# Five scattered tiles on two sums, three row sums combined by DVE and PE, and selection matrices made in quarters

## The reference, cut to what matters

```python
# x: (1024, 256); 16 experts with hidden size 256
logits = x @ router_weight.T + router_bias
top_val, top_idx = jax.lax.top_k(logits, 4)
router_scores = zeros.at[token, top_idx].set(softmax(top_val))
gate_up = einsum('th,ehd->etd', x, gate_up_proj) + bias
out = einsum('etd,edh->eth', (up + 1) * glu(gate), down_proj) + down_bias
out = (out * router_scores.T[:, :, None]).sum(axis=0)      # a sum over experts, per token
result = x + layernorm(out)
```

## Time and profile before

| | us |
|---|---|
| median of 3 runs | 511.5 (510.91, 511.5, 516.53) |
| the profiled execution's own time | 514.36 |
| its span in the trace | 512.6 |

### The profile page before, as it was taken

The page is one execution under the profiler, slowest core; times in us unless marked ns, Lnnn a source line. Parts: engine busy times, 40 slices in busy tenths (PEclk is TensorE's granted clock), DMA queues, the critical chain, the costliest instruction groups (busy, mean ns, idle before and its releaser), DMA issues. The chain is left out here.

```text
span 512.6 us, 11665 instructions
## 1 busy us (share of the span) xinstructions
PE 469.9 (92%) x3466; PEld 439.8 (86%) x3466; DVE 356.6 (70%) x1258; ACT 325.5 (63%) x815; POOL 248.5 (48%) x236
## 2 busy tenths in 40 slices
PE   6699999999999999999999999789889999999933
PEld 3698898999899999999999998588789999998833
DVE  4698788686866686876687797376666767668605
ACT  4878986768586767576676656546458665655402
POOL 1888884444222355435442245016835555554363
PEclk9999999999999999999999999998899999999967
DMA  8357651999400000000365346533655555655742
GB/s 240 108 188 234 213 182 35 374 369 370 159 1 1 22 25 36 23 26 36 127 212 179 127 140 212 165 115 67 139 104 102 93 106 92 105 91 79 160 127 84
DMA packets 63406, 67.49 MB, mean 132 GB/s; under 512 B 4529, under 2 KB 58225, under 8 KB 63345
## 3 DMA queue, kind: packets, MB, share of 16 engines
q1 hardware_dynamic: 54896, 55.79, 34.6%
q0 software_dynamic: 7872, 10.49, 11.8%
q10 hardware_dynamic: 576, 0.46, 0.3%
HBM read 32.63 MB, written 34.10 MB: 130 GB/s over the span
## 5 line engine op out<-in xcount | busy, mean ns | idle before, releaser
L514 POOL TENSOR_TENSOR by_sin<-by_sin,rope_sin 128x512 f32<-128x512 f32 x64 | 82.4, 1288 | 148.5 <-ACT by_sin L659 148.5
L1522 PE MATMUL bank<-xgT,gu_now 128*128 128x128 f32 x752 | 95.1, 281 | 3.6 <-ACT xgT L659 1.7
L659 ACT ACTIVATE by_sin<-bank 64x512 f32<-64x512 f32 x128 | 75.7, 592 | 34.1 <-PE bank L1324 32.6
L612 POOL DMA_INDIRECT sum_d<-y,xg x44 | 68.5, 1558 | 58.7 <-ACT y L787 55.1
L1522 PEld LDWEIGHTS bank<-xgT,gu_now 128*128 128x128 f32 x752 | 90.9, 198 | 5.0 <-DVE gu_now L1143 3.8
L681 ACT ACTIVATE prob<-score,row_bias 128x128 f32<-128x128 f32 (+1 forms) x128 | 57.1, 447 | 47.2 <-DVE row_bias L971 47.1
L1324 PE MATMUL bank<-xT_h,qk_h 128*128 128x256 f32 x256 | 77.5, 303 | 4.3 <-DVE qkT L961 1.7
L971 DVE CUSTOM_DVE_ANT_0 score<-bank,mask 128x128 f32<-128x128 f32 (+1 forms) x128 | 40.3, 351 | 52.2 <-issue 52.2
L1324 PE MATMUL bank<-xT_h,qk_l 128*128 128x256 f32 x256 | 72.2, 282 | 0.0
L1324 PE MATMUL bank<-xT_l,qk_h 128*128 128x256 f32 x256 | 72.1, 282 | 0.0
L1324 PEld LDWEIGHTS bank<-xT_h,qk_h 128*128 128x128 f32 x256 | 48.8, 191 | 5.1 <-POOL qk_l L499 3.4
(11 more groups left out here) (182 smaller groups left out, 1178.6 us busy)
## 6 DMA issues: line engine op xcount, KB each, us to landing
rows_d<-blank SPq DMA_DIRECT2D x32, 576.0 KB, 7.5
gu_w<-_L_ffn_gate_up_proj_dram SPq DMA_DIRECT2D x16, 512.0 KB, 5.7
xg<-rows_d SPq DMA_DIRECT2D x47, 144.0 KB, 2.6
dn_w<-in_L_ffn_down_proj_dram SPq DMA_DIRECT2D x16, 256.0 KB, 3.0
sum_d<-blank SPq DMA_DIRECT2D x2, 1152.0 KB, 9.9
raw_qk<-in_L_attn_wq_dram SPq DMA_DIRECT2D x16, 128.0 KB, 3.6
raw_qk<-in_L_attn_wk_dram SPq DMA_DIRECT2D x16, 128.0 KB, 3.7
raw_v<-in_L_attn_wv_dram SPq DMA_DIRECT2D x8, 256.0 KB, 2.7
```

The lines of the kernel that those rows point to most:

```text
L514: pool.tensor_tensor(v, v, rope_sin[:, :].unsqueeze(1).broadcast_to([P, 2, T]), ALU.mult).then_inc(pool_sin, 1)
L612: pool.indirect_dma_start(out=sum_d[i % SUMS], out_offset=bass.IndirectOffsetOnAxis(ap=xg[:, i % XG, TOKEN:TOKEN + 1].bitcast(U32), axis=0 ...
L659: return sc.activation(out, in_, ACT.Copy)
L1522: m = pe.matmul(ps_gu[i % 2][:, (2 * s + r) * P:(2 * s + r + 1) * P], gu_now[:, i % 2, k, s, r * P:(r + 1) * P], xgT[:, i % XT, k, :], sta ...
```

## The change

In the loop and at its end:

- Scatters 39 to 43 go to sums 0 and 1 in turn (`HOME`), so each of 41 to 43 waits for the scatter two before it, no longer three before. Sum 2 has its last scatter with tile 38, and SP loads it to `sum_a` as soon as that has landed and the row loads are issued.
- The last two sums are loaded in four parts each (two for `sum_b` before).
- The additions on POOL go. DVE adds `sum_b` to `sum_a` (`add_two`); PE adds that and, by an own pair of products, `sum_c` (`add_sum`).
- PE does the products of the first two late tiles for all units ahead of any sum, then unit by unit those of the third tile and the two sums.
- The token numbers of the late tiles come by three small loads of their own (`late_token`, 8 bytes a row), and the 0/1 comparisons are made in quarters of 256 columns, one after each of tiles 20 to 31.
- `down(46)` writes to another PSUM bank (that of `gate_up(45)`), and waits for DVE's reading of it rather than for tile 44's late rows. Tile 44's `late_low` stands in the loop, after `gated(46)`.
- The last token tile's output is stored by ACT on its own queue, in a DMA of 128 KB, beside SP's.

```diff
+        ps_out = [ps_y[i % 2] for i in range(TILE_MAX - 1)] + [ps_gu[TILE_MAX % 2]]
...
-        ENDING = [(LAST + k) % SUMS for k in range(SUMS)]
+        TWO = LAST - 5
+        HOME = [i % SUMS if i < TWO else (TWO + (i - TWO) % 2) % SUMS for i in range(LAST)]
+        def added(i):
+            return 16 * HOME[:i + 1].count(HOME[i])
...
-            for i in range(EARLY + 3, TILE_MAX):
+            for i in range(EARLY + 3, EARLY + XG):
                 load_rows(i)
-            for i, to, signal in ((ENDING[0], sum_a, dma_first), (ENDING[1], sum_b, dma_second)):
-                sp.wait_ge(dma_sum[i], 16 * ((LAST - 1 - i) // SUMS + 1))
-                for u in range(2):
-                    sp.dma_start(to[:, 4 * u:4 * u + 4, :], sum_rows[i][:, 4 * u:4 * u + 4, :]).then_inc(signal[u], 16)
-            sp.wait_ge(dma_sum[ENDING[2]], 16 * ((LAST - 1 - ENDING[2]) // SUMS + 1))
-            for u in range(4):
-                sp.dma_start(sum_c[:, 2 * u:2 * u + 2, :], sum_rows[ENDING[2]][:, 2 * u:2 * u + 2, :]).then_inc(dma_third[u], 16)
-            for u in range(4):
+            for j in range(LATE):
+                row = sp.value_load(entry(LAST + j, 1), min_val=0, max_val=BLANK)
+                sp.dma_start(late_token[:, j, :], rows_d[bass.ds(row, P), TOKEN:TOKEN + 2].bitcast(I32)).then_inc(dma_token, 16)
+            for i in range(EARLY + XG, TILE_MAX):
+                load_rows(i)
+            sp.wait_ge(dma_sum[HOME[TWO - 1]], added(TWO - 1))
+            for u in range(2):
+                sp.dma_start(sum_a[:, 4 * u:4 * u + 4, :], sum_rows[HOME[TWO - 1]][:, 4 * u:4 * u + 4, :]).then_inc(dma_first[u], 16)
+            for i, to, signal in ((LAST - 2, sum_b, dma_second), (LAST - 1, sum_c, dma_third)):
+                sp.wait_ge(dma_sum[HOME[i]], added(i))
+                for u in range(4):
+                    sp.dma_start(to[:, 2 * u:2 * u + 2, :], sum_rows[HOME[i]][:, 2 * u:2 * u + 2, :]).then_inc(signal[u], 16)
+            for u in range(3):
                 sp.wait_ge(act_moe, 2 * u + 2)
                 sp.dma_start(out_rows[:, 2 * u:2 * u + 2, :], sum_b[:, 2 * u:2 * u + 2, :]).then_inc(dma_out, 16)
-            sp.wait_ge(dma_out, 16 * 4)
+            sp.wait_ge(act_moe, TILES - 1)
+            sp.dma_start(out_rows[:, TILES - 2, :], sum_b[:, TILES - 2, :]).then_inc(dma_out, 16)
+            sp.wait_ge(dma_out, 16 * 5)
...
-                    pool.wait_ge(dma_sum[i % SUMS], 16 * (i // SUMS))
-                pool.indirect_dma_start(out=sum_d[i % SUMS], out_offset=bass.IndirectOffsetOnAxis(
+                    pool.wait_ge(dma_sum[HOME[i]], added(i) - 16)
+                pool.indirect_dma_start(out=sum_d[HOME[i]], out_offset=bass.IndirectOffsetOnAxis(
                     ap=xg[:, i % XG, TOKEN:TOKEN + 1].bitcast(U32), axis=0), in_=y[:, i % YR, :], in_offset=None,
-                    compute_op=ALU.add).then_inc(dma_sum[i % SUMS], 16)
+                    compute_op=ALU.add).then_inc(dma_sum[HOME[i]], 16)
...
-            def add_second(u):
-                pool.wait_ge(dma_first[u // 2], 16)
-                pool.wait_ge(dma_second[u // 2], 16)
-                tiles = slice(2 * u, 2 * u + 2)
-                pool.tensor_tensor(sum_a[:, tiles, :], sum_a[:, tiles, :], sum_b[:, tiles, :], ALU.add).then_inc(pool_first, 1)
-            def add_third(u):
-                pool.wait_ge(dma_third[u], 16)
-                pool.wait_ge(pool_first, u + 1)
-                tiles = slice(2 * u, 2 * u + 2)
-                pool.tensor_tensor(sum_a[:, tiles, :], sum_a[:, tiles, :], sum_c[:, tiles, :], ALU.add).then_inc(pool_whole, 1)
             for u in range(4):
-                add_second(u)
-            add_third(0)
-            add_third(1)
-            add_third(2)
-            power("moe", 0)
-            add_third(3)
-            for u in range(1, 4):
                 power("moe", u)
...
+            sc.wait_ge(act_moe, TILES)
+            sc.dma_start(out_rows[:, TILES - 1, :], sum_b[:, TILES - 1, :]).then_inc(dma_out, 16)
...
-            def rows_to_tokens(j):
-                i = LAST + j
-                dve.wait_ge(dma_xg[i % XG], 16 * (i // XG + 1))
-                chain(dve.tensor_copy(token[:, j:j + 1], xg[:, i % XG, TOKEN:TOKEN + 1].bitcast(I32)))
-                chain(dve.tensor_scalar(from_end[:, j, :], full_edge[:, :], token[:, j:j + 1], None, ALU.subtract))
-                dve.tensor_tensor(turn[:, j, :, :], from_end[:, j, :].unsqueeze(2).broadcast_to([P, TILES, P]),
-                                  countdown[:, :].unsqueeze(1).broadcast_to([P, TILES, P]), ALU.is_equal).then_inc(dve_turn, 1)
+            def token_rows():
+                dve.wait_ge(dma_token, 16 * LATE)
+                dve.tensor_copy(token[:, :], late_token[:, :, 0]).then_inc(dve_token, 1)
+                dve.wait_ge(dve_token, 1)
+                dve.tensor_tensor(from_end[:, :, :], full_edge[:, :].unsqueeze(1).broadcast_to([P, LATE, TILES]),
+                                  token[:, :].unsqueeze(2).broadcast_to([P, LATE, TILES]), ALU.subtract).then_inc(dve_token, 1)
+                dve.wait_ge(dve_token, 2)
+            def which_token(j, u):
+                tiles = slice(2 * u, 2 * u + 2)
+                dve.tensor_tensor(turn[:, j, tiles, :], from_end[:, j, tiles].unsqueeze(2).broadcast_to([P, 2, P]),
+                                  countdown[:, :].unsqueeze(1).broadcast_to([P, 2, P]), ALU.is_equal).then_inc(dve_turn, 1)
...
-                dve.scalar_tensor_tensor(out=late_l[:, j, :], in0=ps_y[i % 2][:, 0:M], scalar=xg[:, i % XG, bass.ds(e + M, 1)],
...
                     experts[i + 1] = place_gu(i + 1)
                 clamp(i, experts[i])
                 gated(i)
-                if LAST - 4 <= i < LAST - 4 + LATE:
-                    rows_to_tokens(i - LAST + 4)
-            for j in range(LATE):
+                if i == EARLY + 10:
+                    token_rows()
+                if EARLY + 10 < i <= EARLY + 10 + 4 * LATE:
+                    which_token((i - EARLY - 11) // 4, (i - EARLY - 11) % 4)
+                if i - 2 >= LAST:
+                    late_low(i - 2 - LAST, experts[i - 2])
+            for j in range(LATE - 2, LATE):
                 late_low(j, experts[LAST + j])
+            def add_two(u):
+                dve.wait_ge(dma_first[u // 2], 16)
+                dve.wait_ge(dma_second[u], 16)
+                tiles = slice(2 * u, 2 * u + 2)
+                dve.tensor_tensor(sum_a[:, tiles, :], sum_a[:, tiles, :], sum_b[:, tiles, :], ALU.add).then_inc(dve_two, 1)
+            for u in range(4):
+                add_two(u)
...
                 e = pe.value_load(entry(i, 0), min_val=0, max_val=E - 1)
                 pe.wait_ge(dve_act, i + 1)
-                if i >= 2:
+                if i == TILE_MAX - 1:
+                    pe.wait_ge(dve_up, i)
+                elif i >= 2:
                     pe.wait_ge(act_y, i - 1)
-                if i - 2 >= LAST:
-                    pe.wait_ge(dve_late, i - 1 - LAST)
+                    if i - 2 >= LAST:
+                        pe.wait_ge(dve_late, i - 1 - LAST)
                 for r in range(2):
-                    m = pe.matmul(ps_y[i % 2][:, 0:M], act[:, i % AR, r, :],
+                    m = pe.matmul(ps_out[i][:, 0:M], act[:, i % AR, r, :],
...
                 if i > EARLY:
                     down(i - 2)
-            def add_late(u, j, first=False, last=False):
-                pe.wait_ge(dve_turn, j + 1)
+            def add_late(u, j, first=False):
+                pe.wait_ge(dve_turn, 4 * j + u + 1)
                 pe.wait_ge(dve_late, j + 1)
                 for s in range(2):
                     for rows in (late_h, late_l):
-                        m = pe.matmul(ps_sum[u][:, s * M:(s + 1) * M], turn[:, j, 2 * u + s, :], rows[:, j, :],
-                                      start=first and s == 0 and rows is late_h, stop=last and s == 1 and rows is late_l,
-                                      skip_group_check=True)
+                        pe.matmul(ps_sum[u][:, s * M:(s + 1) * M], turn[:, j, 2 * u + s, :], rows[:, j, :],
+                                  start=first and s == 0 and rows is late_h, stop=False, skip_group_check=True)
+            def add_sum(u, rows, last=False):
+                for s in range(2):
+                    m = pe.matmul(ps_sum[u][:, s * M:(s + 1) * M], ident[:, :], rows[:, 2 * u + s, :], start=False,
+                                  stop=last and s == 1, skip_group_check=True)
                 return m
-            def add_sums(u):
-                pe.wait_ge(pool_whole, u + 1)
-                for s in range(2):
-                    pe.matmul(ps_sum[u][:, s * M:(s + 1) * M], ident[:, :], sum_a[:, 2 * u + s, :], start=False, stop=False,
-                              skip_group_check=True)
             pe.wait_ge(act_xgT, TILE_MAX)
+            for j in range(LATE - 1):
+                for u in range(4):
+                    add_late(u, j, first=j == 0)
```

(10 more changed lines are left out.)

17 lines of the change are left out of this document (10 added, 7 removed).

## The result

| | before | changed |
|---|---|---|
| median of 4 runs, us | 511.21 (510.12 to 516.53) | 504.85 (502.79 to 505.05) |
| profiled execution, us | 514.36 | 502.79 |
| its span, us | 512.6 | 501.0 |
| ratio (95% interval) | | 0.986 (0.981 to 0.990) |

The forecast was 501.6 us with a range of 499.8 to 505.5. The median lies inside, 3.2 us above the forecast. The two profiled executions differ by 11.6 us, the medians by 6.4; the difference between those two numbers is one of the things to explain.

A forecast was written before the change was run, and what follows sets the result against it. PE bounds the loop; the end waits for scatter, load and addition in series. First statistics 8.9, later units 0.75 and store 0.2 sum to 9.85 us, off 511.5: 501.6 us, range 499.8 to 505.5.

The forecast's parts named there:

- The bound moved to PE: Tail from `down(46)` on: PE's own work sets it at full clock; loads, additions and store lie beside it.
- The first statistics, 24.4 us: After the first unit's sums: first statistics 24.4 us behind scatter 38's issue, at 489.3 against 498.17, 8.9 us earlier.
- `sum_c`'s first quarter, 3.3 us: Load of the last sum: its first quarter takes 3.3 us, as before, landing between 486.9 and 489.5.
- Quarters, 1.4 us: Loop: quarter comparisons fill DVE's gaps at no cost; the whole ones had cost 1.5 us, 1.4 taken as gain.
- No delay of scatter 42: End of loop: scatter 42 not held by scatter 40 beside `sum_a`'s load; 1.3 us kept for the range.
- my first rival: `sum_a`'s load holds up the scatters and the last lands late; gain 8.5 us, 503.0 us; chance 0.17.
- The rival's second half: Last scatter: 43, issued at 479.4, takes 6.9 us to land, so `sum_c` goes at 486.3; chance 0.17 for the whole rival.
- that rival's queue mechanism: Scatters 39 to 41 count as landed only behind `sum_a`'s bytes on the DMA engines; delay 1.3 us; rival's chance 0.17.
- the fourth rival: Chain of two sums makes it slower: landings of 11.1 us give 517.7 us, deciding from about 9.5 us; chance 0.02.
- The clock: PE after its late products: pauses at most some 2 us, so 2.4 GHz throughout instead of first work at half speed.
- First to last statistics, 6.2 us: Units at the end: 1.9 + 2.1 + 2.2 = 6.2 us from first to last statistics instead of 6.95; 0.75 us gained.
- The split store, 0.2 us: Very end: last store half as large and issued by ACT; gain 0.2 us, between 0 and 0.5.

The follow-up runs named there:

- undisturbed copies: Executions of the changed kernel, unedited, in which PE waits under 0.1 us for `sum_c`; tails 38.32 and 38.50 us, agreeing within 0.2 us.
- the first copy: Changed kernel run again without edit, against the kernel before: ratio 0.983, 502.96 against 512.01 us, tail 38.32 us.
- The experiment on the kernel before: Kernel before plus 34 extra calls of unused products in PE's long wait for the sums: ratio 1.000, tail 45.46 us against 47.64.
- the two copies: Changed kernel run twice more without edit, against the kernel before: ratio 0.983 (502.96 against 512.01 us) and 0.982 (509.99 against 519.41 us).

## Why the prediction was right, and where its terms were off

**The bound moved to PE: right, with one wait left over.** From `down(46)` to the last pair PE works without a pause in the undisturbed copies, and a pair less on PE shortened the tail by its own length. The engine that adds (POOL or DVE) changed nothing, and the order of the loads nothing where `sum_c` was in time. In other executions, the profiled one among them, PE waits 0.4 to 1.1 us for the first quarter of `sum_c`. What the whole shortened chain is worth is the rest of an account: 47.64 less 38.3 to 39.1 is 8.5 to 9.3 us. Of it the 1.4 us of the comparisons and the 1.8 us of the clock are named below, and 5.3 to 6.1 us are left, of them 0.9 to 1.7 us the early load of `sum_a` and 0.5 us the shorter wait before `down(46)` (0.20 us instead of 0.73). The rest was not taken apart by runs.

**The first statistics, 24.4 us: close, partly by luck.** The copies without a wait had 24.28 us. But the 24.4 held 0.4 us of waiting for `sum_c`; the forecast's own sum without it is 24.0. What came instead was a pair of 0.86 us where 0.67 had been taken. In the profiled execution it was 25.07 us.

**`sum_c`'s first quarter, 3.3 us: mis-sized.** In the row that it was taken from, `sum_b` had been on its way for 5.65 us when `sum_c` was issued (482.08 to 487.73); now it had been for 1.94 us. Here the quarter took 5.37 us in the profiled execution and 2.6 to 6.0 in the others.

**Quarters, 1.4 us: right in size, half right in the reason.** Scatter 43 came at 14.53 us instead of 15.89 (1.36 us). The cost of a quarter, none, held. But the step that took the whole comparison alone as what PE waited for was wrong: alone it fits under the cover, and with whole comparisons in the changed kernel the loss goes over the stretched scatters. In the kernel before it was comparison and small steps together.

**No delay of scatter 42: wrong in the profiled execution, right in the copies.** I took none and kept 1.3 us for the range. Scatter 40 landed after 6.07 us, which is near the 6.9 us of my first rival; 42 was held, `sum_b` was issued 0.9 us later than in the first copy, and PE waited 0.53 us. The first statistics were 0.8 us later than in that copy. The rival's second half, a landing of 6.9 us for scatter 43, did not come (3.6 us). Whether scatter 40 was slowed by the load's traffic, or only counted late behind its bytes, as that rival's queue mechanism would have it, no run here tells apart. In the fourth rival the limit of 9.5 us for a landing is miscalculated: by its own terms (467.8 + 3 x 9.0 + 4.3 = 499.1) it is 9.0. Nothing hangs on it.

**The clock: right.** Full until the last product. The experiment on the kernel before gives the price, 1.8 us, which the forecast had inside its terms without separating it.

**First to last statistics, 6.2 us: mis-sized.** It took 6.60. I had 1.86 us of PE's work for a unit and, for two of the three steps, DVE's longer work; the rows show 2.20 us a unit on PE. The two pairs of a unit are not alike: 0.86 us for `sum_a`'s, which follows late products (487.21 to 488.07), and 0.68 for `sum_c`'s (488.07 to 488.75); the other 0.66 are the four late products at 0.165 instead of 0.13 us. The gain was 0.35 us, not 0.75. The kernel before with the clock kept full has 6.58 us there, so even the 0.35 us is the clock's, and the new order of PE's work gained nothing behind the first statistics.

**The split store, 0.2 us: worth nothing.** The forecast took the store for the end of the kernel. In all traces POOL's closing DRAIN of 5.14 us ends behind it.

**From the trace to the median.** The trace's tail gained 8.53 us of the 9.85 forecast: 0.7 short at the first statistics, 0.4 after them, 0.2 at the store. The medians differ by 6.4 us, and what is left is outside the changed code. It goes with the granted clock of TensorE before scatter 38. In the profiled execution of the changed kernel the mean clock was 0.996; in the other three it was 0.988 to 0.990, and their spans are 1.9 to 2.2 us longer. The traces name the place: the routing stage, where the clock drops to 1.2 GHz for a while. In the first copy:

```profile
328.00:330.00 2.00, 1.84 (x7) 0.51 0.02 4
330.00:332.00 2.00, 1.66 (x7) 0.63 0.45 107
```

In six executions scatter 38 comes later the more of such stretches there are: with none at 461.86 us, with 3.41 us at half level at 462.26 and 463.08, with 6.83 at 464.91 (the kernel before), with 10.24 at 465.29, with 13.65 at 466.20. That is about 0.3 us lost for each us at half level, and some 2 of the 3.05 us that the two traces differ ahead of scatter 38. The rest is open, and so is more: in the other seven executions of the changed kernel and its variants, taken on three other chips, scatter 38 comes at 468.4 to 471.1 us with 6.83 to 17.07 us at half level, 2 to 5 us later than this line gives. Something besides the clock differs there, and no run shows what. The forecast subtracted a gain worked out in one execution from a median over executions with other clocks; the two copies, with more runs, gave 9.05 and 9.4 us in medians, near the forecast of 9.9.

## What to carry to other kernels

When a chain of loads and additions ends a kernel, look for work of the fastest engine that needs none of them, put it ahead of them, and let that engine take the last term itself: here the chain then hid behind PE, the adding engine no longer mattered, and of the loads only the first part of the last one did. In the one run that put that part ahead of what was not needed yet, PE did not wait. A pause that such a rebuild removes can give back more than its length, because the work behind it no longer starts at 1.2 GHz (1.8 us here). Look at which instruction ends the span before working on the last store: here it was POOL's, not a DMA. Compare such edits from a common point in the traces: ends differed by 1 us reliably where medians of the runs differed by several us for reasons that lay 100 us earlier.

## What the runs showed of the hardware

- **A scatter that starts while DVE compares is stretched.** POOL's instruction took 1.55 us alone, 1.70 beside a quarter (started 407.31, the quarter 407.17 to 407.59) and 2.50 beside a whole comparison already running (465.29 against 465.15 to 466.37). In the kernel before the comparison began 0.36 us behind the scatter's start (464.91), and the scatter took its 1.55 us. Both stretched ones ended 1.42 us behind the end of DVE's instruction. The Trainium skill, page "SBUF — State Buffer", section "Who interferes with whom", says that DVE and GpSimd share a pair of ports which whoever comes first keeps for its whole instruction. It adds that a DVE instruction with two SBUF inputs contends with a GpSimd instruction that reads SBUF, and infers that one like it does not hold back the writing of DMA descriptors. The trace agrees with the first two: the comparison has two inputs in SBUF, the scatter reads its row numbers there, and it was 0.95 us longer. Which of the scatter's steps was held no run shows, so the inference stands open; such a DVE operation does not leave the scatter as a whole alone.
- **DVE's small steps are stretched beside POOL's additions.** A 128x2 step that takes 0.17 us took 0.77 (497.44 to 498.21) while POOL added from 496.92 to 498.17, and ended with it.
- **A scatter's landing beside a load of 1 MB** took 6.07 us, and 5.68 and 5.84 in two other runs, 4.3 us being the median of all.
- **POOL's closing DRAIN takes 5.14 us** from its last instruction in every trace here, whatever the stores do, and ends 1.1 to 1.3 us behind the last landing.
